# Row maxima taken one and a half groups ahead of the scores instead of two, in an attention and expert kernel

## The chip, the cores and the metric

The kernel runs on one core of a Trainium2 chip. The metric is device time in microseconds (us), from the start of the program to its end. Its engines work side by side and meet through semaphores: TensorE (PE, matmuls), VectorE (DVE), ScalarE (ACT), GpSimd (POOL), and SyncE (SP), which here only issues DMA transfers.

## The reference

Eight batches of 512 tokens with 256 features pass through a cross attention with 16 heads of 16, and then through a layer of eight experts of which each token takes two.

```python
q = _split_heads(_layernorm(x) @ wq.T + bq)
k = _split_heads(ctx @ wk.T + bk)
v = _split_heads(ctx @ wv.T + bv)
attn = softmax(einsum('bhqd,bhkd->bhqk', q, k) * 0.25)
x = x + einsum('bhqk,bhkd->bhqd', attn, v).reshape(B, S, 256) @ wo.T + bo
probs = softmax((_layernorm(x) @ Wg + bg) / 5.0)      # the two largest of 8, normalised: gates
h = gelu(_layernorm(x) @ W1[e] + b1[e])
x = x + sum_e gates[e] * (h @ W2[e] + b2[e])
```

## The kernel before

**Tiling.** The attention is cut into 32 groups, u = 0 to 31: eight batches i, and in each four groups g of four heads. A group is cut into eight slots, p = 0 to 7; a slot is two heads by one block of 128 keys (or queries) by 512. I write (g, p) for a slot of a batch, and batch and slot apart where both matter. The core's work for a group is done twice over:

- The **maxima pass**. `score` (L1448, the matmuls of L1457) puts the scores of 128 queries by 512 keys for two heads into one of three PSUM buffers (`ring`), and DVE's `reduce_max` (L1012) takes the negated row maxima into `negm`. When the group's eight slots are done, a unit called MT turns `negm` (PE, L1492), ACT copies it to `mT` (L903), and SP's `put_max` (L454, the DMA of L458) writes it into an extra row of the query stack `q_st`, 8 KB. The semaphore of that transfer is `m_in`.
- The **scores pass**. `score_t` (L1461, the matmuls of L1470) makes the transposed scores, and since the extra row is multiplied by a row of ones in `k_st`, they come out less the maximum. ACT takes the exponential into `probs` (L944), and `pv` (L1474, L1483) multiplies by the values. The first `score_t` of a group waits for `m_in`.

**What sets the order.** Each engine's program is written out by hand. In each slot PE does `score_t(u, p)`, then the maxima matmuls that `ahead(u, p)` names, then `pv` in slots 0, 2, 4 and 6, then the units that tables give for the slot. Before, `ahead` names slot p of group u + 2; in group 0 it names two in each of the first four slots, to catch up with the twelve made in the prologue (`EARLY`). The three PSUM buffers are handed round in the order of `ring_order`: a matmul pair may start only when the reader of the pair three places earlier is done, so in the steady order the scores of slot p wait for the DVE reduction of slot p - 2, and the maxima of slot p for the exponential of slot p - 1.

**Units.** The tables `PREP`, `NEXT`, `FIRST`, `POST` and `LAST_POST` put the other work into slots: XT and CT (transposes of the queries' and the context's input), K, Q, V (projections), OP (output projection of the batch before), XG and LG (transposes and logits of the routing), PX (ranks of the tokens among the experts' rows), CN (counts). Nearly all of them share one PSUM bank, `ps_x`, and each waits until the engine that empties it has taken the one before (`claim`). On DVE the tables `LN`, `LN2`, `ROUTE` and their LAST forms hold normalisation and routing. In the last batch DVE also makes tables for the expert stage (`first_tables`, L1228, in slots (2, 0), (2, 2) and (2, 4)), which end with `row_tab` (L1253). `row_tab` sets `tab_done`, and ACT waits for that before it copies XG0 to `xgT` (L910), because `xgT` lies in the same memory as the scratch of these tables. Two halves of a weight split (`low_w1`, L1195) stand between them on DVE, four more on POOL (L738).

**Queue of SP.** SP issues its transfers in program order and waits in that order: `put_max`, `load_stack` (k_st and q_st from HBM, L437), `store_parts` (K and Q to HBM, L451), `put_o` and `put_recip` (outputs and reciprocals), `fetch_o`, `load_kv`, `load_x`, weights.

**After the attention** 82 tiles of tokens run through the experts, bound to the order of `turn_x`, `hidden`, `turn_h` and `output` on PE (L1591 to L1627).

## Time and profile before

| | us |
|---|---|
| median of 3 runs | 833.87 |
| the three runs | 827.43, 833.87, 835.49 |
| the profiled execution | 829.04 |
| its span, first to last instruction | 827.3 |
| PE busy | 767.5 (93%) |
| DVE busy | 629.3 (76%) |
| ACT busy | 452.4 (55%) |
| POOL busy | 394.7 (48%) |
| attention: first score of group 0 to last `pv` | 40.2 to about 545 |

All times below count from the first instruction of the profiled execution; 1.7 us of its time lie outside the span. A row of the time line gives the start, the length from there to the end of the last instruction of the piece, the engine (SPq is SP's issuing queue), the line, the operation with what it writes and reads, the count, and in brackets how long the engine stood idle before it and what ended that. PE's matmuls are pipelined, so the next one starts some 0.1 us before the end shown.

### The profile page before, as it was taken

To read this page: it belongs to the slowest core of one execution; us is meant where nothing else is said; L and a number is where in the kernel's file an instruction comes from. 1 tells how busy PE (TensorE), PEld (TensorE's weight loads), DVE (VectorE), ACT (ScalarE), POOL (GpSimd) and SP (SyncE) were. 2 spreads that over 40 slices of the span, in tenths; PEclk is the share of its full clock that TensorE was granted. 3 is DMA by queue.
4 is the path that set the end of the run, shared out by engine and by line. 5 is a ranking of instruction groups with operands and counts; after the bars stand their busy time and mean duration, and the time that the engine had idled before them with its cause. 6 is when DMAs were issued, how large, how long until landed. Compare 5 with 4: busy or idle time off the path is not lost.

```text
span 827.3 us, 16330 instructions
## 1 busy us (share of the span) xinstructions
PE 767.5 (93%) x4698; PEld 459.5 (56%) x4698; DVE 629.3 (76%) x1131; ACT 452.4 (55%) x667; POOL 394.7 (48%) x358
## 2 busy tenths in 40 slices
PE   8599999999999999999999978678999989999995
PEld 4343434544434444444444423247989879998894
DVE  6786678798788798798778787866786887776674
ACT  2166676775775775776765655453345434444441
POOL 6506142446446456455425347654344455443444
PEclk9689999999999999999999979869999999999999
DMA  5766566567667667657467535263454456444441
GB/s 190 232 172 195 129 206 196 154 201 230 172 197 231 170 197 237 161 174 237 134 185 250 160 78 166 85 232 73 77 91 79 73 120 116 74 77 70 73 74 12
DMA packets 90285, 123.66 MB, mean 149 GB/s; under 512 B 15081, under 2 KB 52937, under 8 KB 89817
## 3 DMA queue, kind: packets, MB, share of 16 engines
q1 hardware_dynamic: 75832, 104.74, 43.2%
q0 software_dynamic: 13296, 17.09, 11.9%
q8 instruction: 43, 0.70, 0.4%
q10 hardware_dynamic: 1072, 0.79, 0.3%
q14 instruction: 42, 0.34, 0.2%
HBM read 64.96 MB, written 57.75 MB: 148 GB/s over the span
## 4 chain that ended last, share of the span: by engine, by line
PE 73%; DVE 10%; DMA 6%; issue 4%; ACT 2%; POOL 2%; SPq 0%; DVEq 0%; POOLq 0%; ACTq 0%
PE ps_pv L1483 14%; PE ring L1470 11%; PE ring L1625 9%; PE ring L1607 9%; PE ring L1457 7%; PE ps_x L1511 6%; DMA out<-y_sb,xs 5%; PE ps_x L1529 4%; DVE negm L1012 4%; PE ps_x L1501 3%; PE ps_x L1521 3%; PE ring L1616 3%; PE ps_x L1538 2%; PE ps_pv L1598 1%; ACT probs L944 1%
## 5 line engine op out<-in xcount | busy, mean ns | idle before, releaser
L1012 DVE TENSOR_REDUCE negm<-ring 128x2 f32<-128x1024 f32 x256 | 310.3, 1222 | 76.2 <-PE ring L1457 74.2
L944 ACT ACTIVATE probs<-ring 128x1024 f32<-128x1024 f32 x256 | 260.6, 1024 | 98.4 <-PE ring L1470 98.2
L845 POOL DMA_INDIRECT out<-y_sb,xs x71 | 110.3, 1554 | 138.3 <-DMA out<-y_sb,xs 82.6
L1483 PE MATMUL ps_pv<-probs,v_aug 128*32 128x512 f32 x1024 | 141.4, 625 | 5.3 <-ACT probs L944 5.2
L1470 PE MATMUL ring<-q_st,k_st 64*128 64x512 f32 x512 | 128.9, 503 | 6.5 <-DVE negm L1012 6.5
L1457 PE MATMUL ring<-k_st,q_st 64*128 64x512 f32 x512 | 110.7, 432 | 11.3 <-ACT probs L944 5.2
L1470 PEld LDWEIGHTS ring<-q_st,k_st 64*128 64x128 f32 x512 | 48.6, 188 | 107.7 <-issue 77.2
L973 ACT CAST xsT_hi<-ps_pv 128x256 fp32r<-128x256 f32 x71 | 26.4, 372 | 134.3 <-PE ps_pv L1598 134.3
L716 POOL DMA_INDIRECT xs_dram<-xg,rows x64 | 65.2, 1019 | 56.1 <-DVEq L1180 25.8
L1625 PE MATMUL ring<-w_hi,hT_hi 128*128 x284 | 85.7, 302 | 2.5 <-POOL w_lo L743 2.4
L1625 PE MATMUL ring<-w_lo,hT_hi 128*128 x284 | 80.3, 283 | 0.0
L1625 PE MATMUL ring<-w_hi,hT_lo 128*128 x284 | 79.8, 281 | 0.0
L785 POOL TENSOR_TENSOR v_aug<-v_flat,bv_sb 128x256 f32<-128x256 f32 x32 | 22.9, 733 | 99.5 <-PE ps_pv L1483 89.3
L1368 DVE TENSOR_TENSOR h_pre<-ring,b_sb 128x512 f32<-128x512 f32 x71 | 49.0, 690 | 25.6 <-PE ring L1607 24.2
L1607 PE MATMUL ring<-w_hi,xsT_hi 128*128 x142 | 59.6, 420 | 7.1 <-DVE xsT_lo L1356 6.9
L1457 PEld LDWEIGHTS ring<-k_st,q_st 64*128 64x128 f32 x512 | 50.9, 195 | 25.8 <-DVE negm L1012 8.9
L769 POOL CAST qk_hi<-qk 128x512 fp32r<-128x512 f32 x28 | 17.2, 613 | 89.2 <-ACT qk L897 58.5
L1607 PE MATMUL ring<-w_hi,xsT_lo 128*128 x142 | 57.1, 402 | 0.0
L1607 PE MATMUL ring<-w_lo,xsT_hi 128*128 x142 | 56.9, 401 | 0.0
L1625 PEld LDWEIGHTS ring<-w_hi,hT_hi 128*128 128x128 f32 x284 | 54.0, 190 | 2.9 <-issue 2.9
L1625 PEld LDWEIGHTS ring<-w_lo,hT_hi 128*128 128x128 f32 x284 | 54.0, 190 | 0.0
L1625 PEld LDWEIGHTS ring<-w_hi,hT_lo 128*128 128x128 f32 x284 | 53.8, 189 | 0.0
(194 smaller groups left out, 1236.6 us busy)
## 6 DMA issues: line engine op xcount, KB each, us to landing
k_st<-k_dram SPq DMA_DIRECT2D x64, 192.0 KB
q_st<-q_dram SPq DMA_DIRECT2D x64, 192.0 KB
xs<-xs_dram SPq DMA_DIRECT2D x71, 132.5 KB, 2.2
k_dram<-qk_hi SPq DMA_DIRECT2D x32, 256.0 KB, 2.4
q_dram<-qk_hi SPq DMA_DIRECT2D x32, 256.0 KB, 2.8
o_dram<-oT SPq DMA_DIRECT2D x32, 256.0 KB, 2.7
x_all<-in_x SPq DMA_DIRECT2D x8, 512.0 KB, 4.8
k_dram<-qk_lo SPq DMA_DIRECT2D x16, 256.0 KB, 2.3
```

Of the source, the lines that this page charges most:

```text
L716: pool.indirect_dma_start(out=xs_dram, out_offset=bass.IndirectOffsetOnAxis(ap=rows[:, k, t:t + 1], axis=0), in_=xg[:, t, :], in_offset=No ...
L845: pool.indirect_dma_start(out=out, out_offset=bass.IndirectOffsetOnAxis(ap=xs[j % AHEAD][:, TOKEN:TOKEN + 1].bitcast(I32), axis=0), in_=y_ ...
L944: nc.scalar.activation(probs[:, kt, 2 * jp:2 * jp + 2, :], ring[PLACE["ST", u, p] % RINGS][:], ACT.Exp).then_inc(exp_done, 1)
L1012: nc.vector.tensor_reduce(negm[:, v % 2, :, jp, kt], ring[PLACE["MX", v, p] % RINGS][:], AX.X, ALU.max, negate=True).then_inc(max_free, 1)
L1368: v.tensor_tensor(h_pre[:, j % 2, :], ps_h[j % 2], b1_sb[:, bass.ds(e, 1), :].rearrange("p o h -> p (o h)"), ALU.add).then_inc(f_h_out, 1)
L1457: mm = nc.tensor.matmul(ps[:, h, :], q_st[lo:lo + HALF, 2 * g + jp, kt * P:(kt + 1) * P], k_st[lo:lo + HALF, 2 * g + jp, :], start=True, s ...
L1470: mm = nc.tensor.matmul(ps[:, h, :], k_st[lo:lo + HALF, 2 * g + jp, kt * P:(kt + 1) * P], q_st[lo:lo + HALF, 2 * g + jp, :], start=True, s ...
L1483: mm = nc.tensor.matmul(ps_pv[2 * DH * j:2 * DH * (j + 1), :], v_aug[:, kt, HPG * g + j, :], probs[:, kt, j, :], start=(kt == 0), stop=(kt ...
L1511: mm = nc.tensor.matmul(ps[:, half], w[:, c, f * P:(f + 1) * P], act_t[:, c, half], start=(c == 0), stop=(c == DC - 1))
L1529: mm = nc.tensor.matmul(ps[:, (t % 2) * D:(t % 2 + 1) * D], numT[:, c, t * P:(t + 1) * P], wo_sb[:, c, :], start=(c == 0), stop=(c == DC - 1))
L1607: mm = nc.tensor.matmul(ps_h[j % 2], x[:, j % 2, c, :], w[:, bass.ds(e, 1), c, :].rearrange("p o h -> p (o h)"), start=(n == 0), stop=(n = ...
L1625: mm = nc.tensor.matmul(ps_y[j % 2][:, 0:D], h[:, j % 2, c, :], w[:, bass.ds(e, 1), c, :].rearrange("p o d -> p (o d)"), start=(n == 0), s ...
```

## The change

`ahead` now names slot p + 4 of group u + 1 in the first half of a group and slot p - 4 of group u + 2 in the second half, for every group, so that group 0 has eight maxima slots instead of twelve, and group 30 has four where it had none. MT of the next group stands in slot 4 instead of slot 0. The context's transposes CT0 and CT1 move from (3, 4) and (3, 6) to (3, 0) and (3, 2). In the first batch CT0, CT1 and XT0 move ahead, in the last batch OP2, OP3 and three normalisation steps move back by a slot or so. On SP `put_max` moves behind the transfers that stood after it.

```diff
-NEXT = {(2, 7): "XT0", (3, 1): "XT1", (3, 4): "CT0", (3, 6): "CT1"}
+NEXT = {(2, 7): "XT0", (3, 0): "CT0", (3, 1): "XT1", (3, 2): "CT1"}
-FIRST = {(0, 1): "CT0", (0, 2): "CT1", (0, 3): "K0a", (0, 4): "XT0", ...
+FIRST = {(0, 0): "CT0", (0, 1): "CT1", (0, 2): "XT0", (0, 3): "K0a", ...
-LAST_POST = {(1, 1): "OP0", (1, 3): "OP1", (1, 4): "OP2", (1, 5): "OP3",
+LAST_POST = {(1, 1): "OP0", (1, 3): "OP1", (1, 5): "OP2", (1, 6): "OP3",
-LAST_LN2 = {(1, 4): "stats0", (1, 6): "stats1", (1, 7): "sums"}
+LAST_LN2 = {(1, 5): "stats0", (1, 7): "stats1", (2, 0): "sums"}
...
-    if p == (2 if u == 0 else 0) and u + 1 < G:
+    if p == NP // 2 and u + 1 < G:
         out.append(("MT", u + 1))
...
 def ahead(u, p):
-    if u == 0:
-        rest = [(1, q) for q in range(NP // 2, NP)] + [(2, q) for q in range(NP)]
-        return rest[2 * p:2 * p + 2] if p < NP // 2 else rest[p + NP // 2:p + NP // 2 + 1]
-    return [(u + 2, p)] if u + 2 < G else []
+    v, q = (u + 1, p + NP // 2) if p < NP // 2 else (u + 2, p - NP // 2)
+    return [(v, q)] if v < G else []
...
-                put_max(i, 1)
...
                 if i > 0:
+                    put_max(i, 1)
                     fetch_o(i - 1, 1)
...
-                put_max(i, 2)
                 if more:
                     load_stack(i + 1, 0)
                 put_o(NG * i)
                 if more:
                     store_parts("Q", i + 1, 1)
+                if i > 0:
+                    put_max(i, 2)
+                if more:
                     store_parts("K", i + 1, 1)
...
-                put_max(i, 3)
...
                 put_recip(i, 0)
+                put_max(i, 3)
                 fetch_o(i, 0)
...
-                    put_max(i + 1, 0)
                     load_stack(i + 1, 2)
                 put_o(NG * i + 2)
+                if more:
+                    put_max(i + 1, 0)
```

Three places of the order follow. First PE in slots 0 to 3 of group 0, where ring<-k_st,q_st is a maxima matmul and ring<-q_st,k_st a scores matmul. Before:

```order
L1470 MATMUL ring<-q_st,k_st 128x512 x2
L1457 MATMUL ring<-k_st,q_st 128x512 x4
L1470 MATMUL ring<-q_st,k_st 128x512 x2
L1457 MATMUL ring<-k_st,q_st 128x512 x4
L1501 MATMUL ps_x<-ident,kv 128x128 x4
L1470 MATMUL ring<-q_st,k_st 128x512 x2
L1457 MATMUL ring<-k_st,q_st 128x512 x4
L1483 MATMUL ps_pv<-probs,v_aug 32x512 x4
L1492 MATMUL ps_x<-ident,negm 16x128
L1501 MATMUL ps_x<-ident,kv 128x128 x4
```

Of the change (its lines stand five lower in the file):

```order
L1475 MATMUL ring<-q_st,k_st 128x512 x2
L1462 MATMUL ring<-k_st,q_st 128x512 x2
L1506 MATMUL ps_x<-ident,kv 128x128 x4
L1475 MATMUL ring<-q_st,k_st 128x512 x2
L1462 MATMUL ring<-k_st,q_st 128x512 x2
L1506 MATMUL ps_x<-ident,kv 128x128 x4
L1475 MATMUL ring<-q_st,k_st 128x512 x2
L1462 MATMUL ring<-k_st,q_st 128x512 x2
L1488 MATMUL ps_pv<-probs,v_aug 32x512 x4
L1506 MATMUL ps_x<-ident,xn 128x128 x4
```

Each slot has lost one maxima pair, the transposes stand one or two slots earlier, and MT has left slot 2.

Second, SP from `put_recip` of the batch before (r_dram<-den) to the stacks of the next batch, in the first two groups of a batch. Before, the maxima's transfer (q_st<-mT) of group 1 has gone out ahead of these rows and that of group 2 is the seventh:

```order
L474 DMA r_dram<-den 128x32
L451 DMA k_dram<-qk_hi 128x512
L451 DMA k_dram<-qk_lo 128x512
L451 DMA k_dram<-qk_hi 128x512
L485 DMA numT<-o_dram 128x1x512
L490 DMA recT<-r_dram 128x1x512
L451 DMA q_dram<-qk_hi 128x512 x2
L451 DMA q_dram<-qk_lo 128x512
L458 DMA q_st<-mT 2x8x128
```

Of the change:

```order
L472 DMA r_dram<-den 128x32
L449 DMA k_dram<-qk_hi 128x512
L449 DMA k_dram<-qk_lo 128x512
L449 DMA k_dram<-qk_hi 128x512
L456 DMA q_st<-mT 2x8x128
L483 DMA numT<-o_dram 128x1x512
L488 DMA recT<-r_dram 128x1x512
L449 DMA q_dram<-qk_hi 128x512 x2
L449 DMA q_dram<-qk_lo 128x512
L435 DMA k_st<-k_dram 48x2x512 x2
```

The transfer of group 1 now stands right behind three stores of K, and that of group 2 has moved on behind stacks, output and the last stores of Q.

Third, DVE in the last batch, in slots (2, 0) to (2, 3), around the expert tables. Before:

```order
L1240 TENSOR_TENSOR done_n<-ends 128x7
L1195 TENSOR_TENSOR w_lo<-w_sb,w_hi 128x1024
L1242 TENSOR_TENSOR past<-tile_no,ends 128x328
L1243 TENSOR_TENSOR past_n<-past,done_n 128x328
L1244 TENSOR_REDUCE e_of<-past 128x41
L1245 TENSOR_REDUCE first_of<-past_n 128x41
L1195 TENSOR_TENSOR w_lo<-w_sb,w_hi 128x1024
L1044 RECIPROCAL den<-den 128x32
L1247 TENSOR_SCALAR e_tab<-e_of 128x41
```

Of the change:

```order
L1245 TENSOR_TENSOR done_n<-ends 128x7
L1017 TENSOR_REDUCE negm<-ring 128x2
L1200 TENSOR_TENSOR w_lo<-w_sb,w_hi 128x1024
L1017 TENSOR_REDUCE negm<-ring 128x2
L1247 TENSOR_TENSOR past<-tile_no,ends 128x328
L1248 TENSOR_TENSOR past_n<-past,done_n 128x328
L1249 TENSOR_REDUCE e_of<-past 128x41
L1250 TENSOR_REDUCE first_of<-past_n 128x41
L1017 TENSOR_REDUCE negm<-ring 128x2
L1200 TENSOR_TENSOR w_lo<-w_sb,w_hi 128x1024
L1049 RECIPROCAL den<-den 128x32
L1252 TENSOR_SCALAR e_tab<-e_of 128x41
```

Three maxima of group 31 stand between the table pieces, and a fourth ahead of them, in slot (2, 0).

## Rows read from the trace of the kernel before

**Rows 1.** Windows by stage: length, then PE, PEld, DVE, ACT, POOL busy, clock, DMA

```profile
180.00:240.00 60.00, 59.44 (x369) 27.05 (x367) 49.22 (x86) 40.91 (x56) 31.64 (x32) 1.00 0.66 197
473.00:511.00 38.00, 30.64 (x170) 11.66 (x169) 29.63 (x56) 18.64 (x23) 21.20 (x19) 0.82 0.42 121
511.00:546.00 35.00, 22.20 (x145) 7.85 (x142) 28.88 (x66) 19.27 (x24) 18.34 (x12) 0.86 0.40 137
```

**Rows 2.** PE's waits from 475 to 546 us: total us, times, longest

```profile
PE ps_x L1501 <- ACT xgT L910: 5.3, 1, 5.3
PE ring L1470 <- DVE negm L1012: 4.2, 3, 2.2
PE ps_x L1529 <- DVE numT L1048: 2.9, 1, 2.9
```

**Rows 3.** Time line of the first groups

```profile
37.73 9.14 DVE L1012 TENSOR_REDUCE negm<-ring 128x2 f32<-128x1024 f32 x8 [1.29 <-PE ring L1457]
40.23 0.79 PE L1470 MATMUL ring<-q_st,k_st 64*128 64x512 f32 x2 [0.43 <-DVE negm L1012]
45.39 1.12 PE L1501 MATMUL ps_x<-ident,kv 128*128 128x128 f32 x4
60.50 0.50 PE L1470 MATMUL ring<-q_st,k_st 64*128 64x512 f32 x2
```

**Rows 4.** Windows of PE alone: length, busy, granted clock, DMA share, GB/s

```profile
42.00:44.00 2.00, 1.66 (x8) 0.50 1.06 224
48.00:50.00 2.00, 1.65 (x13) 0.91 0.25 81
```

**Rows 5.** Time line of a middle batch, PE and SP

```profile
239.20 0.46 SPq L451 DMA_DIRECT2D k_dram<-qk_hi  x1
239.29 1.07 PE L1483 MATMUL ps_pv<-probs,v_aug 128*32 128x512 f32 x8
240.28 0.50 PE L1470 MATMUL ring<-q_st,k_st 64*128 64x512 f32 x2
240.62 0.40 PE L1457 MATMUL ring<-k_st,q_st 64*128 64x512 f32 x2
242.86 0.50 PE L1470 MATMUL ring<-q_st,k_st 64*128 64x512 f32 x2
252.58 0.46 SPq L451 DMA_DIRECT2D q_dram<-qk_lo  x1
258.72 0.49 PE L1470 MATMUL ring<-q_st,k_st 64*128 64x512 f32 x2
```

**Rows 6.** DMA issues, 236 to 245 us: KB each, us from issue to landing

```profile
k_dram<-qk_lo SPq DMA_DIRECT2D x1, 256.0 KB, 2.4
q_dram<-qk_lo SPq DMA_DIRECT2D x1, 256.0 KB, 6.6
r_dram<-den SPq DMA_DIRECT2D x1, 16.0 KB, 2.2
```

**Rows 7.** Time line of the last batch, group 30

```profile
510.61 0.74 DVE L1075 BATCH_NORM_STATS2 stats<-x_all 128x6 f32<-128x256 f32 x2
511.27 1.21 DVE L1012 TENSOR_REDUCE negm<-ring 128x2 f32<-128x1024 f32 x1
519.47 0.28 DVE L1247 TENSOR_SCALAR e_tab<-e_of 128x41 int32<-128x41 f32 x1
520.72 2.27 DVE L1250 TENSOR_TENSOR first_of<-tile_no,first_of 128x41 f32<-128x41 f32 x1
525.30 2.28 DVE L1253 SCALAR_TENSOR_TENSOR row_tab<-e_of,first_of 128x41 int32<-128x41 f32 x1
520.56 9.27 POOL L738 TENSOR_TENSOR w_lo<-w_sb,w_hi 128x1024 fp32r<-128x1024 f32 x4
527.68 0.58 ACT L910 COPY xgT<-ps_x 128x512 f32<-128x512 f32 x1 [7.76 <-DVE row_tab L1253]
528.33 1.12 PE L1501 MATMUL ps_x<-ident,xg 128*128 128x128 f32 x4 [5.30 <-ACT xgT L910]
```

## Prediction: what the change does to the time

> **What bounds the kernel now.** I read the windows by stage first. From batch 1 to batch 6 the reader sees PE busy for 59.4 of 60 us at the full clock (level 2.4 GHz), with DVE at 49, ACT at 41 and POOL at 32 [rows 1]. PE's work binds there, and a change that leaves that work alone and only shifts it can save at most the missing 0.6 us in 60. The last batch is different. From 473 to 511 us PE is busy for 31 of 38 us at a mean clock of 0.82, and from 511 to 546 for 22 of 35 at 0.86: here PE waits, and falls to the half level (1.2 GHz) between its waits. PE's waits of that part are, longest first, 5.3 us for ACT's copy to xgT, 4.2 us in three waits for a maximum on DVE, 2.9 us for the normalised outputs, again DVE [rows 2]. The 5.3 us are no matter of ACT: ACT had itself stood idle for 7.8 us until DVE ended row_tab [rows 7]. So in the last batch DVE's queue sets the pace, and in group 30 the path is DVE to row_tab, ACT's copy, PE's XG1. The beginning is a third case: eight reductions stand back to back from 37.7 us, 1.14 us each (9.14 by 8), the first scores wait for one of them, and group 0 takes from 40.23 to 60.50, 20.3 us [rows 3]. A middle group takes a quarter of the 60 us.
>
> **The change, part by part.** The sum of maxima slots stays at 256; four of them (4 x 2 matmuls, 4 reductions) leave slots 0 to 3 of group 0, and four come into slots 0 to 3 of group 30. All groups between have eight before and after. So there are two terms, of opposite sign, and one question about waits.
>
> *Start.* At the full clock a scores or a maxima pair costs PE 0.34 us (240.28 to 240.62), `pv` 1.0 (239.29 to 240.28), half a projection 0.95 (half of what lies between 240.96 and 242.86) [rows 5], and four transposes 0.56 (half of the 1.12 at the half level) [rows 3]. Group 0 after the change holds 16 pairs, three `pv`, four sets of transposes and three half projections: 5.4 + 3.0 + 2.2 + 2.9 = 13.5 us. Before it held four pairs more, 14.9 us, and took 20.3: 5.4 lost. Of these 4.1 are the half clock from 40.2 to about 48.4 (in 42 to 44 us the clock is 0.50, in 48 to 50 us it is 0.91 [rows 4]), and 1.3 are waits. The clock came back after PE had worked without a gap since the transposes at 45.39. Now CT0 stands in slot 0, where PE waited for DVE's second pair, and PE should be without gaps from about 42.4, which is 3 us earlier. If the clock comes back that much earlier, at 45, the half level costs 2.4 us, and with 1.0 of waits the group takes 16.9: 3.4 us saved. If it comes back at the same time as before, some 18.4: 1.9 saved. The lowest price is that of the four pairs alone, 1.4. I take 3.0, nearer to the upper end, since the clock follows the gaps in every row that I have.
>
> *Group 30.* Four reductions of 1.21 us [rows 7] come into DVE's queue between the end of group 29 and row_tab, which is 4.9 us. The move of OP3 by a slot brings one pair of layer norm statistics into it as well, 0.7 us [rows 7]. PE and ACT don't hide this, they are the ones who wait. Does DVE have a gap there that takes it up? No: from 511.27 to 527.58 its instructions stand without one. What can change the price is POOL. While POOL runs its four weight splits, from 520.56 to 529.83, DVE's small operations take as long as one of POOL's: first_of 2.27 us and row_tab 2.28, for 41 elements a partition [rows 7]. POOL starts about 2 us later now (its normalisation waits for DVE's sums, which come behind one reduction and the statistics), so it ends at about 531.8, and DVE, 5.6 us later, does its last eight table operations from 525.1 on: three of them under POOL at 2.27 each, to 531.9, then five in the open at the 0.28 of e_tab, to 533.3. So row_tab ends 5.6 us later; if the second split half and the reciprocal are slowed by POOL too, 6.9. I take 5.8 and keep 4.9 and 6.9. Everything behind the copy to xgT (XG1, logits, routing, the last scatter, the experts) keeps its order and moves with it.
>
> The Trainium skill, GPSIMD Engine Reference, section Key points, says that GpSimd shares its SBUF interfaces with VectorE and that the two get into each other's way when a DVE instruction has two SBUF inputs or is in a 2-port mode. The trace agrees, by the 2.27 us of first_of. By this rule the reductions, which read PSUM, would keep their 1.21 us under POOL, and the split half would not: that speaks for the upper end of this term.
>
> *Middle.* MT moves from slot 0 to slot 4, CT0 and CT1 take the two slots 4 and 6 places earlier, and every slot keeps about the sum it had. The order of the three buffers is the same. I put this at nothing; its cover is that PE has work in every slot, and at most 0.5 us a batch is there to be had. What is new is the time left to `put_max`. MT ended eight slots ahead of the first scores of its group, now four. In group 0 of a batch SP gets to it behind `put_recip` and three stores of K, the last issued from 239.20 to 239.66, and the scores that need it stand at 242.86 [rows 5]. It would be issued at 239.7, so it has 3.1 us to land. The rows nearest to it are 16 KB in 2.2 us and the store of K just ahead in 2.4 [rows 6], so 0.7 us remain. In group 1 it goes out behind the last store of Q (252.58 to 253.04) and is needed at 258.72: 5.7 us [rows 5], against 2.2 of the small transfer, or 6.6 of the slowest store of Q [rows 6]. In both I take the small transfer's 2.2 us, so no wait; the other end is in the rivals. Behind `put_max` on SP stand the fetches, each 0.6 us later, and DVE asks for those only many slots later. The earlier loads of the stacks get half a group more; no wait for them stands in the middle before, so that gives nothing.
>
> Sum: -3.0 + 5.8 + 0 = +2.8 us, from 829.04 to 831.8. The profiled execution stands 4.8 us below the median of the three runs, 833.87. The mean of all four is 831.5, and the same shift from there gives 834.3. I predict 834, about no change: work has gone from a place where it cost 3 to one where it costs nearly 6.
>
> **The rivals.**
>
> *Late maxima.* The 8 KB wait in the queue for the stores ahead of them. For it: 768 KB of K go out right ahead, and a store of Q landed only after 6.6 us [rows 6]. Against it: the store of K just ahead took 2.4. It decides from a landing of over 3.1 us in group 0. With 4.6 there, midway between 2.4 and 6.6, PE stands 1.5 us; with 6.6 in group 1 another 0.9 us; over six batches 14 us: 834.3 + 14 = 848, slower by 1.7%. The Trainium skill, DMA: Bandwidth & Descriptors, section Queues, rings and completion order, says that on each DMA engine the descriptors are consumed in the order of the ring. By this rule the 8 KB come behind all of the 768 KB, which is this rival; whether the wait gets long enough no row shows. Chance 0.16.
>
> *DVE's extra work is hidden.* The copy to xgT doesn't decide, or POOL's splits end before DVE's last operations and give back what the reductions cost (three operations at 2.3 us would fall to 0.28, -6 us). Against it: POOL starts later too. Then only the start counts: 831.5 - 3 = 828.5. Chance 0.12.
>
> *The change doesn't do at the start what it should.* The clock comes back no earlier and other waits take the place of the four pairs. Then + 5.8 alone: 837. Chance 0.10.
>
> *The last batch loses its half clock.* With the work standing otherwise, PE's gaps from 473 to 511 us fall elsewhere. At a mean of 0.82 these 38 us lose 6.8 us to the clock [rows 1]; with the 4.2 us of waits for maxima [rows 2] the most is 11 us, and with the start and the tables 834.3 - 11 = 823. Against it: groups 28 and 29 keep their count of reductions and all of their routing on DVE. Chance 0.08.
>
> **How the numbers follow.** The forecast, within some 3 us of 834, has 0.54. About 1% (8.3 us) is what a measurement of this kernel tells from no change, since its own runs lie 8 us apart. Within it of 833.87 are the forecast, the hidden case and the lost start: 0.76. Slower by over 1%: the late maxima, 0.16. Faster by over 1%: the last batch's clock, 0.08. The range for 8 in 10 takes in 828.5 and 837 with the bounds of the terms (start 1.4 to 3.4, tables 4.9 to 6.9) and the scatter of the runs: 826 to 843.
>
> **What would show it.** Right if group 0 runs in 17 to 18.5 us and the clock is full before 46 us; if the middle windows keep PE at over 59 of 60 us with no wait for DMA at L1475; and if, counted from the first scores of group 28, row_tab ends 5 to 7 us later than before. Wrong if PE waits at the first scores of a group (late maxima), if row_tab's delay is under 4 us (hidden), or if a middle batch changes its length by more than 0.5 us, which no term of mine explains.

## The result and the profile after

The changed kernel takes 837.38 us, the median of 9 runs (835.1 to 840.23), against 833.87 of before in 9 runs (827.43 to 835.9). The ratio, by which all differences here are told, is 1.0056 with a 95% interval of 1.0032 to 1.008 (the two medians alone give 1.0042, inside it): slower by 0.3 to 0.8%, which is within 1%, as forecast (834, range 826 to 843). Its profiled execution took 838.08 us with a span of 836.4. That of before, 829.04, was a quick one among its runs, so the two traces lie 9.1 us apart where the ratio gives 4.7. I come back to those 4 us.

Lines of the changed kernel stand five lower in the file than those of before (L1012 is L1017), those of SP's queue two higher (L458 is L456), and in the experiments they are a little further off. First the windows by stage, with the columns of [rows 1]; the last stage is 5 us longer than in [rows 1] and the clock in it 0.67 in place of 0.86. Part of that is no work of the change: in the start alone, an experiment below that keeps the last batch of before, the clock from 511 to 551 us is 0.69 as well. In the middle window PE is busy for 58.65 of 60 us, where the prediction wanted over 59.

```profile
120.00:180.00 60.00, 59.98 (x350) 26.87 (x352) 47.12 (x79) 40.70 (x55) 22.08 (x24) 0.97 0.57 172
180.00:240.00 60.00, 58.65 (x368) 27.08 (x361) 49.17 (x80) 41.30 (x55) 31.04 (x32) 1.00 0.65 198
473.00:511.00 38.00, 29.93 (x165) 11.62 (x164) 28.73 (x53) 18.76 (x23) 21.29 (x19) 0.78 0.27 87
511.00:551.00 40.00, 27.72 (x134) 9.94 (x135) 31.94 (x63) 18.09 (x22) 16.87 (x11) 0.67 0.36 119
```

**The start** is as forecast. Its time line answers to [rows 3], the two windows of PE alone to [rows 4]:

```profile
39.82 0.80 PE L1475 MATMUL ring<-q_st,k_st 64*128 64x512 f32 x2 [0.42 <-DVE negm L1017]
41.59 1.11 PE L1506 MATMUL ps_x<-ident,kv 128*128 128x128 f32 x4
57.29 0.50 PE L1475 MATMUL ring<-q_st,k_st 64*128 64x512 f32 x2
```

```profile
42.00:44.00 2.00, 2.00 (x9) 0.50 1.07 226
46.00:48.00 2.00, 2.00 (x16) 0.88 1.11 335
```

CT0 now stands at 41.59 in what was a gap, PE is busy for all of 42 to 44 us, the clock is back before 48, and group 0 takes 17.5 us instead of 20.3.

**The middle** is not. Here are PE's waits from 180 to 473 us, of the changed kernel (total us, times, longest):

```profile
PE ps_x L1497 <- DVE negm L1017: 4.8, 5, 1.2
PE ring L1462 <- ACT probs L949: 1.4, 2, 0.7
PE ps_x L1516 <- DVE row_of L1174: 0.3, 2, 0.2
```

and of the kernel before:

```profile
PE ring L1470 <- DVE negm L1012: 1.8, 4, 0.5
PE ring L1457 <- ACT probs L944: 1.4, 2, 0.7
```

MT (L1497) waits once in each batch, in slot (1, 4). The time line of one batch, DVE and PE, shows what it waits for:

```profile
248.39 1.11 DVE L1179 TENSOR_TENSOR row_k<-row_of,oh 128x32 f32<-128x32 f32 x1
250.32 3.57 DVE L1017 TENSOR_REDUCE negm<-ring 128x2 f32<-128x1024 f32 x3
249.41 1.06 PE L1488 MATMUL ps_pv<-probs,v_aug 128*32 128x512 f32 x8
251.69 0.27 PE L1497 MATMUL ps_x<-ident,negm 128*16 128x128 f32 x1 [1.22 <-DVE negm L1017]
```

DVE takes out the ranks of PX from slot (1, 2) on and then runs three reductions back to back. MT needs the first of the three, that of slot (1, 3). Before, the scores of the next slot had to wait for DVE at the same place, but only 0.5 us.

**Group 30** answers to [rows 7]:

```profile
524.52 9.81 DVE L1200 TENSOR_TENSOR w_lo<-w_sb,w_hi 128x1024 fp32r<-128x1024 f32 x1
535.45 0.20 DVE L1255 TENSOR_TENSOR first_of<-tile_no,first_of 128x41 f32<-128x41 f32 x1
535.91 0.20 DVE L1258 SCALAR_TENSOR_TENSOR row_tab<-e_of,first_of 128x41 int32<-128x41 f32 x1
523.97 9.27 POOL L743 TENSOR_TENSOR w_lo<-w_sb,w_hi 128x1024 fp32r<-128x1024 f32 x4
536.22 0.59 ACT L915 COPY xgT<-ps_x 128x512 f32<-128x512 f32 x1 [9.31 <-DVE row_tab L1258]
536.86 1.12 PE L1506 MATMUL ps_x<-ident,xg 128*128 128x128 f32 x4 [6.67 <-ACT xgT L915]
```

DVE's second split half takes 9.81 us, from just behind the start of POOL's four splits to just behind their end; elsewhere such a half takes 1.2 us. The table operations behind it are back at 0.2 us. Counted from the first scores of group 28, row_tab ends at 62.0 us (536.11 less 474.10), before at 53.95 (527.58 less 473.63): 8.1 us later. Only 6.8 of them lie behind the first scores of group 30.

| first scores of group, counted from those of group 0, after less before | us |
|---|---|
| 1 | -2.8 |
| 8 | -3.2 |
| 28 | +0.9 |
| 31 | +8.9 |
| last scores of group 31 | +11.1 |

So against this one execution of before the start gave 3 us, the middle took back 4, the tables 8, and group 31 another 2; behind the attention 2 of these came back, since the spans lie 9.1 us apart. The last of these steps is not the change's doing: group 31 of before was a quick one. From its first scores to its last it took 12.5 us there, 14.6 in the changed kernel, and 17.5 in the start alone, whose group 31 is the same work as before.

The other traces show how much such a reading is worth. From the first scores of group 8 to those of group 28, the stretch of the middle, the eight executions whose middle is that of before took 306.9 to 310.7 us (before itself 308.3), the four with the middle of the change 312.4 to 313.3. So the 4 us of the middle stand clear of the scatter; a difference of 2 us between two single traces would not.

### The profile page after: what moved, and what is told of

It is laid out like the page before. It is cut to its first block, busy times and chain, and to the rows that moved or that the text cites. A ratio compares the mean times of both kernels' runs of the same rounds, so it can differ in the third digit from the quotient of the medians.

```text
span 836.4 us, 16330 instructions
## 1 busy us (share of the span) xinstructions
PE 772.8 (92%) x4698; PEld 460.0 (55%) x4698; DVE 631.9 (76%) x1131; ACT 456.4 (55%) x667; POOL 393.1 (47%) x358
## 4 chain that ended last, share of the span: by engine, by line
PE 73%; DVE 10%; DMA 7%; issue 4%; ACT 2%; POOL 2%; SPq 1%; POOLq 1%; DVEq 0%; ACTq 0%
PE ps_pv L1488 14%; PE ring L1475 11%; PE ring L1612 9%; PE ring L1630 9%; PE ring L1462 7%; PE ps_x L1516 5%; DMA out<-y_sb,xs 5%; PE ps_x L1534 4%; DVE negm L1017 4%; PE ps_x L1506 3%; PE ps_x L1526 3%; PE ring L1621 3%; PE ps_x L1543 2%; PE ps_pv L1603 1%; DMA recT<-r_dram 1%
## 5 line engine op out<-in xcount | busy, mean ns | idle before, releaser
L1017 DVE TENSOR_REDUCE negm<-ring 128x2 f32<-128x1024 f32 x256 | 311.4, 1223 | 82.5 <-PE ring L1462 79.0
L1488 PE MATMUL ps_pv<-probs,v_aug 128*32 128x512 f32 x1024 | 146.1, 644 | 2.5 <-ACT probs L949 2.5
L1475 PE MATMUL ring<-q_st,k_st 64*128 64x512 f32 x512 | 132.3, 515 | 5.6 <-DVE negm L1017 5.6
L1475 PEld LDWEIGHTS ring<-q_st,k_st 64*128 64x128 f32 x512 | 49.7, 191 | 111.1 <-issue 82.7
```

The costliest lines, as they stand in the source:

```text
L1017: nc.vector.tensor_reduce(negm[:, v % 2, :, jp, kt], ring[PLACE["MX", v, p] % RINGS][:], AX.X, ALU.max, negate=True).then_inc(max_free, 1)
L1475: mm = nc.tensor.matmul(ps[:, h, :], k_st[lo:lo + HALF, 2 * g + jp, kt * P:(kt + 1) * P], q_st[lo:lo + HALF, 2 * g + jp, :], start=True, s ...
L1488: mm = nc.tensor.matmul(ps_pv[2 * DH * j:2 * DH * (j + 1), :], v_aug[:, kt, HPG * g + j, :], probs[:, kt, j, :], start=(kt == 0), stop=(kt ...
```

## The experiments

All comparisons are with the kernel before, run beside each experiment; a difference in us is one of ratios, with 0.001 for 0.83 us. Each ratio is uncertain by 0.002 to 0.0035, so a difference between two experiments by some 3 us. In the diffs, three dots stand for parts left out.

### The start alone

```diff
...
-    if u == 0:
-        rest = [(1, q) for q in range(NP // 2, NP)] + [(2, q) for q in range(NP)]
-        return rest[2 * p:2 * p + 2] if p < NP // 2 else rest[p + NP // 2:p + NP // 2 + 1]
-    return [(u + 2, p)] if u + 2 < G else []
+    return MAXIMA[u, p]
...
```

`MAXIMA` gives each slot one pair, and two in (1, 7), (2, 1), (3, 3) and (3, 5) of batch 0. The parts left out give batch 0 the unit tables, the place of MT and the order of `put_max` of the change.

> The kernel before with the first batch of the change alone: one maxima pair in a slot of group 0 in place of two, CT0, CT1 and XT0 ahead, MT of the next group in slot 4, and put_max in the order of the change. The four maxima pairs that group 0 no longer makes are made up in slots (1, 7), (2, 1), (3, 3) and (3, 5) of the first batch; from batch 1 on everything is the kernel before. My theory (the start saves 2.8 us of group 0, and the four pairs cost 4 x 0.34 = 1.4 us of PE where they now stand): faster than before by 1.4 to 2.8 us, and from the first scores of group 0 to those of group 4 1.4 to 2.8 us less. Rival (the gain of the start is only shifted into the rest of the first batch, where the DVE is as late as it was): no difference from before, under 0.5 us at the first scores of group 4.

830.99 us, ratio 0.9974 (0.9952 to 0.9997). In the trace group 0 is 2.2 us shorter, but at the first scores of group 4 only 0.2 us are left of it: the four pairs that were made up in batch 0 cost all of it there. Two later kernels with the same start agree: 0.1 and 0.2 us at group 4, 0.5 and 0.6 at group 8. The time says 2.2 us faster (0.3 to 4.0), the traces under 1, so what the start is worth by itself stays open between them. What is settled is that its gain in the changed kernel (2.8 us at group 1, 3.2 at group 8) exists because the four pairs are left out of batch 0, and that they have to be paid in some other place.

### The four reductions of group 30 alone

```diff
-    if p == (2 if u == 0 else 0) and u + 1 < G:
+    if p == (2 if u == 0 else NP // 2 if u == G - 2 else 0) and u + 1 < G:
...
+    if u == G - 3:
+        return [(u + 2, p)] if p < NP // 2 else []
+    if u == G - 2:
+        return [(u + 1, p + NP // 2)] if p < NP // 2 else []
     return [(u + 2, p)] if u + 2 < G else []
...
```

In the part left out `put_max` of group 31 moves behind `put_recip`.

> The kernel before with the end of the change alone: the last four maxima stand in the first half of group 30 instead of the second half of group 29, MT of group 31 in slot 4, its put_max behind put_recip; all else, LAST_POST and LAST_LN2 too, is the kernel before. My theory as the trace of the changed kernel has mended it: four reductions of 1.21 us come ahead of row_tab, the second split half on DVE falls into the four splits of POOL and is held until they end. Then row_tab ends 7 to 9 us later, counted from the first scores of group 28, that split half takes over 8 us instead of 1.2, and the time is 5 to 8 us above before. By the prediction's sum: row_tab 4.9 to 6.2 us later and no long split half. Rival (it was the shift of OP2, OP3 and the normalisation steps or the clock, not the reductions): under 3 us in both.

832.73 us, ratio 1.0001 (0.9976 to 1.0026): no change, and row_tab ends 3.1 us later (57.0 from the first scores of group 28). My theory and the prediction's sum both missed; the rival, that it was the shift and not the reductions, had said under 3 us in both, and came within 0.1 us. Time line of DVE, PE and POOL:

```profile
518.85 1.72 DVE L1249 TENSOR_TENSOR past<-tile_no,ends 128x328 f32<-128x328 f32 x1
520.60 2.53 DVE L1250 TENSOR_TENSOR past_n<-past,done_n 128x328 f32<-128x328 f32 x1
525.37 3.36 DVE L1202 TENSOR_TENSOR w_lo<-w_sb,w_hi 128x1024 fp32r<-128x1024 f32 x1
525.60 0.37 PE L1499 MATMUL ps_x<-ident,negm 128*16 128x128 f32 x1 [4.05 <-DVE negm L1019]
531.27 0.66 PE L1508 MATMUL ps_x<-ident,xg 128*128 128x128 f32 x4 [0.92 <-ACT xgT L917]
517.86 9.78 POOL L745 TENSOR_TENSOR w_lo<-w_sb,w_hi 128x1024 fp32r<-128x1024 f32 x4
```

Without the shift of the normalisation steps POOL starts its splits at 517.86, ahead of most of the table. They then hold three DVE operations for some 5 us in all, not one for 8.6, and end at 527.6; of the wait at XG1 0.9 us remain of 5.3. A new wait of 4.05 us at MT has come in its place.

### The whole end

The edit just shown and, with it, OP2, OP3 and the normalisation steps as in the change:

```diff
-LAST_POST = {(1, 1): "OP0", (1, 3): "OP1", (1, 4): "OP2", (1, 5): "OP3",
+LAST_POST = {(1, 1): "OP0", (1, 3): "OP1", (1, 5): "OP2", (1, 6): "OP3",
-LAST_LN2 = {(1, 4): "stats0", (1, 6): "stats1", (1, 7): "sums"}
+LAST_LN2 = {(1, 5): "stats0", (1, 7): "stats1", (2, 0): "sums"}
```

> The kernel before with the whole end of the change: the four reductions in group 30, as run alone, and with them OP2, OP3 and the three normalisation steps a slot or so later. The reductions alone left the time where it was (1.0001); the changed kernel stands 3.4 us above the same kernel with its end undone. Theory (the shifts bring DVE's split half to the point where POOL's four splits begin, so that it is held to their end): a split half of over 8 us, row_tab 7 to 9 us later than before, the time 2 to 5 us above before. Rival (it was the meeting with the middle, not the shifts): the split half stays under 4 us and the time within 1 us of before.

840.53 us, ratio 1.0066 (1.0033 to 1.01), 5.5 us slower; row_tab ends 5.6 us later (59.5). DVE, POOL and PE:

```profile
523.75 9.83 DVE L1202 TENSOR_TENSOR w_lo<-w_sb,w_hi 128x1024 fp32r<-128x1024 f32 x1
523.21 9.29 POOL L745 TENSOR_TENSOR w_lo<-w_sb,w_hi 128x1024 fp32r<-128x1024 f32 x4
536.12 1.11 PE L1508 MATMUL ps_x<-ident,xg 128*128 128x128 f32 x4 [6.69 <-ACT xgT L917]
```

So the four reductions alone don't bring the split half to the start of POOL's run, and with the shift they do. The shift reads like a detail of the diff, and adding it took the loss from nothing to 5.5 us. The shift without the reductions was not run. The twelve runs of this kernel lie further apart than those of the others (832.5 to 844.2 us), which nothing here explains.

### The change with its end undone

The start and middle of the change; the four pairs are caught up in batch 6, and batch 7 stands as before but for the order on SP.

```diff
...
-    if p == NP // 2 and u + 1 < G:
+    if p == (NP // 2 if u < G - NG else 0) and u + 1 < G:
...
```

> The changed kernel with its end undone: four maxima pairs are caught up in slots (1, 7), (2, 1), (3, 3) and (3, 5) of batch 6, and batch 7 has the maxima, MT, output projection and normalisation steps in the slots of the kernel before. Start and middle are those of the change. Each part alone, as run, gives -2.2 us for the start and 0 for the four reductions in group 30, while the whole change gives +4.7 against the 832.9 of before: some 7 us are in the middle or in how the parts meet. Theory (the middle costs 4 to 5 us by its waits at MT): 834.5 to 836, that is 1.5 to 3 us above before and 1.5 to 3 below the changed kernel. Rival (the middle costs nothing, as predicted, and the loss is the meeting of three late DVE pieces in the last batch): 830 to 831.5, as with the start alone.

834.02 us, ratio 1.0013 (0.9989 to 1.0037). That is 1.1 us above before and 3.3 above the start alone, and 3.6 below the changed kernel (1.0056 less 1.0013). The intervals are about 2 us wide to each side, so the point values decide only together with the traces. In that of this kernel MT waits 3.5 us in five batches, and from group 8 to group 28 it loses 4.9 us; the four traces with the middle of the change lose 4.1 to 4.9 there, the seven experiments without it -1.4 to +2.4. The middle costs 3 to 5 us.

```profile
PE ps_x L1511 <- DVE negm L1031: 3.5, 5, 1.2
```

### MT one slot later

MT of group 2 stands in (1, 5), in batches 2 to 7:

```diff
-    if p == NP // 2 and u + 1 < G:
+    if p == NP // 2 + (g == 1 and i > 1) and u + 1 < G:
```

> The changed kernel with MT of the next group in slot (1, 5) instead of (1, 4), for batches 2 to 7. In the changed kernel PE stands there for 0.6 to 1.2 us in each of these batches until DVE has made the maxima before it, 4.8 us in batches 2 to 6 together, right behind the ranks (PX) that DVE takes out in (1, 2). If it is MT that pays for this, the waits at MT are gone and the time falls by 3 to 5 us, as against the changed kernel. Rival (DVE is late there for everybody, and the scores of slots 5 and 6 wait instead, as they do in the kernel before): the waits move to the scores, at most 1 us in all is gained.

844.25 us, ratio 1.0127 (1.0097 to 1.0157): not faster but 5.9 us slower than the changed kernel. PE in the same batch:

```profile
254.00 0.51 PE L1475 MATMUL ring<-q_st,k_st 64*128 64x512 f32 x2 [1.06 <-DVE negm L1017]
255.75 1.13 PE L1534 MATMUL ps_x<-wo_sb,numT 128*128 128x256 f32 x4 [0.81 <-issue]
```

The wait has moved to the scores of the next slot, and MT now stands right in front of OP0, which needs the same bank ps_x and waits 0.8 us until ACT has emptied it. (The profile names ACT at one of these five waits and gives "issue", no releaser, at the other four.) The rival was right about the first, and nobody had the second. The waits of the five batches come to 2.3 us more than in the changed kernel, while this trace loses 5.6 us more from group 8 to group 28; the rest goes with a lower clock, 0.98 from 120 to 473 us against 0.99. So MT in (1, 4) is not itself the cause: DVE is late there, and whoever asks it next pays.

### DVE's split halves behind the tables

In the kernel before and in the changed kernel:

```diff
-LAST_LOW_W1 = {(2, 1): 6, (2, 3): 7}
+LAST_LOW_W1 = {(2, 5): 6, (2, 7): 7}
```

> The kernel before, with the two halves of the weight split on DVE (low_w1) moved from slots (2, 1) and (2, 3) to (2, 5) and (2, 7) of the last batch, that is behind the expert tables. If POOL's splits and the split halves are what the tables wait for, row_tab ends 6 to 8 us earlier than before (two halves of 1.2 us are gone from ahead of it, and it ends before or soon after POOL starts, so that the 2.3 us operations fall to 0.3), PE's wait of 5.3 us at XG1 is gone or under 1 us, and the time falls by 3 to 6 us; the split halves themselves may take up to 9 us behind the tables. Rival (the chain behind the tables, not the tables, is what the end waits for, or the held split half makes the later operations of DVE just as late): row_tab is earlier but the time changes by less than 1 us.

> The changed kernel with the same move: the two halves of the weight split on DVE in slots (2, 5) and (2, 7) of the last batch. If the 9.8 us split half is what made group 30 some 8 us later instead of 5.8, row_tab ends at least 8 us earlier than in the changed kernel and the time falls by 5 to 9 us, more than the same move brings in the kernel before. Rival (the four reductions alone set the delay): row_tab earlier by the 2.5 us of the two halves, and the time by about 2 us.

The kernel before with this edit: 831.35 us, ratio 0.9967 (0.9946 to 0.9988), row_tab 5.5 us earlier (48.5), a little under what was expected of both. The wait at XG1 is gone, and another has come: PE's longest wait for probs is 6.7 us, where it was 1.1. The changed kernel with this edit: 835.57, ratio 1.0028 (1.0005 to 1.005), 2.3 us below the changed kernel (within what two such ratios leave open), row_tab 3.5 us earlier. Here the rival came nearer, for a reason it did not name. DVE and POOL:

```profile
521.81 8.51 DVE L1252 TENSOR_SCALAR e_tab<-e_of 128x41 int32<-128x41 f32 x1
521.01 9.27 POOL L743 TENSOR_TENSOR w_lo<-w_sb,w_hi 128x1024 fp32r<-128x1024 f32 x4
```

With the split half gone, e_tab is held instead, 8.5 us for an operation of 0.28 us. So the size of the DVE operation is not what makes the hold long.

### POOL waits for row_tab

```diff
                 if i == B - 1:
+                    pool.wait_ge(tab_done, 1)
                     for e in range(2, E - 2):
                         low_w1(e)
```

In the changed kernel, in the kernel before, and in the kernel before with the start of the change:

> The changed kernel with one more wait: POOL begins its four weight splits of the last batch (L743) only when row_tab is made (tab_done). The tables are then made with POOL idle. If POOL's splits are what holds DVE's split half for 9.8 us, that half takes 1.2 us, row_tab ends 8 to 9 us earlier than in the changed kernel (at 53 to 54 us from the first scores of group 28), and PE's wait of 6.7 us at XG1 is under 1 us; the time falls by 3 to 7 us, less than row_tab gains, since POOL's splits now fall on the DVE's later steps and end some 4 us later. Rival (DVE itself is slow there, POOL only happens to run): the split half stays above 5 us and the time changes by under 1 us.

> The kernel before with POOL's four splits waiting for row_tab, and nothing of the change. With the start it gave 828.4, 4.8 us below before, of which 2.2 are the start's by its own run. If the two add, this one is 2 to 3.5 us below before, row_tab ends at 48 to 49 us from the first scores of group 28, and one routing operation of DVE (ld) is held for about 1.9 us later on. Rival (they help each other, since the half clock of group 31 hangs on both): under 1.5 us.

> A version meant to beat both: the kernel before with the start of the change alone (as run above, 2.2 us faster) and with POOL's four splits waiting for row_tab. In the kernel before three table operations take 2.3 us each under POOL's splits in place of 0.2, so row_tab should end 6 us earlier, at 48 to 49 us from the first scores of group 28. If the end waits for row_tab, the time is 824 to 828, 5 to 8 us below before. Rival (as with the weight split moved behind the tables, 5.5 us at row_tab give only 2 to 3 us of time, because POOL's splits then hold DVE's later steps): 827.5 to 830.

The changed kernel with the wait: 832.44 us, ratio 0.9992 (0.9969 to 1.0015), 5.3 us below the changed kernel. The split half takes 1.22 us, row_tab ends at 53.2, and the wait at XG1 is gone:

```profile
525.13 1.22 DVE L1201 TENSOR_TENSOR w_lo<-w_sb,w_hi 128x1024 fp32r<-128x1024 f32 x1
527.93 0.20 DVE L1259 SCALAR_TENSOR_TENSOR row_tab<-e_of,first_of 128x41 int32<-128x41 f32 x1
528.21 12.14 POOL L743 TENSOR_TENSOR w_lo<-w_sb,w_hi 128x1024 fp32r<-128x1024 f32 x4 [3.59 <-DVE row_tab L1259]
```

This shows the cause: DVE is held by POOL's run, not by its own work. The kernel before with the wait: 831.29, ratio 0.9979 (0.9959 to 1.0), 1.7 us faster and so between what the theory and the rival had said; its row_tab ends at 49.3, 4.7 us earlier, and ld is held for the 1.9 us that were expected. With the start as well: **828.36 us, ratio 0.994 (0.9909 to 0.997)**, 5 us below before and 9.7 below the changed kernel, and the lowest time of this study. The gains of the start (2.2) and of the wait (1.7) by themselves add up to 3.9, which is the same within the intervals. Its row_tab ends at 49.3. It is not the 8 us of the best case, and its trace shows the rival at work; DVE, POOL and PE:

```profile
521.83 0.20 DVE L1277 SCALAR_TENSOR_TENSOR row_tab<-e_of,first_of 128x41 int32<-128x41 f32 x1
532.39 1.89 DVE L1138 TENSOR_TENSOR ld<-lg,lmax 128x32 f32<-128x32 f32 x1
522.11 12.11 POOL L761 TENSOR_TENSOR w_lo<-w_sb,w_hi 128x1024 fp32r<-128x1024 f32 x4 [0.88 <-DVE row_tab L1277]
536.42 1.94 PE L1507 MATMUL ps_pv<-probs,v_aug 128*32 128x512 f32 x8 [4.75 <-ACT probs L968]
```

POOL's splits now take 12.1 us in place of 9.3, with DVE's later casts and splits running between them, and ld is held for 1.9.

### Two splits behind the scatter

```diff
-                    for e in range(2, E - 2):
+                    for e in range(2, 4):
                         low_w1(e)
...
                     scatter(i - 1)
+                    for e in range(4, E - 2):
+                        low_w1(e)
```

> The start of the change and POOL's wait for row_tab, as in the version that beat both, but two of POOL's four splits behind the scatter of batch 6. In that version PE waits 4.8 us for probs, ACT 5.4 us for the routing operation ld, and DVE for POOL's splits, two weight splits and ld together about 8 us. With only two splits there these waits shrink to under 2 us, and the time falls by another 2 to 4 us, to 825 to 826.5. Rival (the other two splits now fall into the end of the attention or the start of the experts, where PE needs all eight of them): no gain, or up to 4 us lost.

831.95 us, ratio 0.9974 (0.9953 to 0.9994): 2.8 us above the version it was made from, so the rival was right. The attention itself ends some 8 us earlier (last scores at 534.0, in the version it was made from at 542.5), and then PE stands before the first expert matmul:

```profile
547.10 4.64 POOL L761 TENSOR_TENSOR w_lo<-w_sb,w_hi 128x1024 fp32r<-128x1024 f32 x2
551.88 0.79 PE L1633 MATMUL ring<-w_hi,xsT_hi 128*128 x1 [13.96 <-POOL w_lo L761]
```

POOL stood idle for 11.6 us in front of that scatter. A version that used those for the two splits might keep part of the 8 us; it was not run.

### Maxima that are really late

The changed kernel, with put_max of group 1 behind the fetches and the stores of Q:

```diff
                 if i > 0:
-                    put_max(i, 1)
                     fetch_o(i - 1, 1)
                 if more:
                     store_parts("Q", i + 1, 0)
+                if i > 0:
+                    put_max(i, 1)
```

> The changed kernel with put_max of group 1 behind the fetches and the first stores of Q in batches 1 to 7: the rival of the late maxima, made to happen. In the changed kernel it is issued at 238.65 and the scores that need it stand at 241.31 without a wait; here it is issued at about 241.7. If a landing takes 2.2 us as the 16 KB beside it did, PE waits 2.5 to 3.5 us at the first scores of group 1 in each of batches 1 to 6, and the time is 15 to 22 us above the changed kernel, 852 to 860. If it queues behind the stores ahead of it, 6 to 7 us a batch and over 870. Rival (the scores have slack elsewhere and PE catches up): under 5 us.

867.6 us, ratio 1.0407 (1.0372 to 1.0441), 29 us above the changed kernel; more than the 15 to 22 of my own theory, less than the other end. SP and PE, and PE's waits from 180 to 490 us:

```profile
252.08 0.56 SPq L456 DMA_DIRECT2D q_st<-mT  x1
256.77 0.79 PE L1476 MATMUL ring<-q_st,k_st 64*128 64x512 f32 x2 [5.12 <-DMA q_st<-mT]
```

```profile
PE ring L1476 <- DMA q_st<-mT: 23.5, 5, 5.4
```

The 8 KB take 4.7 us from their issue (252.08 to 256.77), not 2.2: they have 512 KB of fetches and three stores of Q ahead of them. The row of the scores behind the wait is 0.79 us long, as at the half level, against 0.50 in a middle batch of before [rows 5]. The Trainium skill, DMA: Bandwidth & Descriptors, section Queues, rings and completion order, says that each DMA engine takes descriptors in ring order; the 4.7 us agree with that, but one later landing doesn't show it. In the changed kernel itself put_max goes out at 238.65 and the scores of group 1 start at 241.31 without a wait, so it landed within 2.7 us there, behind the 768 KB of K. No matmul of L1475 waits for a DMA in any batch, but this was near: the weight load (PEld) of these very scores names the transfer as what came last. Its 0.76 us of idle stand in another batch too, without a releaser, so no time was lost:

```profile
241.31 0.19 PEld L1475 LDWEIGHTS ring<-q_st,k_st 64*128 64x128 f32 x2 [0.76 <-DMA q_st<-mT]
```

## Why the prediction came out as it did

**The time.** Within 1% of before, inside the range, and the two terms have the signs that I gave them. The sum was +2.8 us; the ratio gives +4.7 (2.7 to 6.7). That it comes this near is in part luck: in group 30 a wrong working led to the right size, and the middle, where a step failed, is small.

**Start, -3.0.** Right: 2.8 us in group 0, with the full clock before 48 us as against about 48.4, and PE without gaps from 41.59 on. The test "full clock before 46" was missed by a little: 44 to 46 us is still at the half level, 46 to 48 at 0.88. A slip of the sum changes nothing: with the same 1.0 us of waits the second case gives 18.6 us for the group, not 18.4. What the start is worth by itself is less sure, since its four pairs have to be paid elsewhere; I had booked that payment under group 30.

**Group 30, +5.8.** The path (DVE, row_tab, ACT's copy, XG1) and the size of the loss were right for the end as a whole: 5.5 us in time and 5.6 at row_tab, run by itself. In the changed kernel row_tab was 8.1 us later, beyond my upper bound of 6.9 and the 5 to 7 of my test; 6.8 of these lie in group 30 and 1.2 in the two groups before it. The 1.2 may be scatter: in the six experiments whose work in these two groups is that of before, they took 0.1 to 2.6 us longer than in the execution that I compare with. The 6.8 are firm, since in all three traces with the tables of before row_tab ends 16.7 to 16.8 us behind the first scores of group 30, and they lie inside my bounds. But the working was wrong in its middle: "three of them under POOL at 2.27 each, to 531.9, then five in the open". No operation of the tables was slowed to 2.27 in the changed kernel. The split half, for which together with the reciprocal I had allowed at most another 1.1 us, was held for all of POOL's 9.3, and everything after it ran in the open. POOL itself began 2.9 us later, counted from group 28, where I had taken 2. I had carried over the pattern of [rows 7], one DVE operation let through after each of POOL's, as if it were a price by the operation. And the part of the diff that I costed at 0.7 us, the shift of OP3 and the statistics, was what, on top of the reductions, brought the half there; the four reductions by themselves made row_tab 3.1 us later and cost no time that could be measured (1.0001, 0.9976 to 1.0026).

**Middle, 0.** This step failed. "I put this at nothing; its cover is that PE has work in every slot": PE's work is no cover for a unit that stands in PE's own order and waits. MT needs the maxima of the slot just before it, in slot 4 as in slot 0; but slot (1, 4) lies behind the PX of (1, 2), for which DVE does seven small operations, and slot (1, 0) doesn't. The waits grew from 1.8 to 5.1 us in five batches, and by time the middle cost 3.3. The text named the test that shows it, a middle batch longer by over 0.5 us: that was so (0.8 a batch from group 8 to group 28, waits and half clock together, though unevenly: 2.2 in the first, next to nothing in the last two).

**The rivals.** Late maxima: not in this kernel, whose transfer landed within 2.7 us where I had counted 3.1 to spare; how near that was the last experiment shows, where an issue 3 us later, behind more transfers, cost 29 us. I had taken 4.6 us as its midway landing, and the one in that experiment took 4.7; that the two are so near is chance, for the queue ahead was another one. Hidden DVE work: refuted for the change, near the truth for the reductions alone. A start that does nothing: refuted for group 0; by itself its worth is open. A better half clock in the last batch: it didn't come. From 473 to 511 us the clock was 0.78 in place of 0.82, and the 0.67 behind it is near the 0.69 and 0.70 of the start alone and of the change with its end undone, both with the last batch's work as before.

**The 4 us between the traces.** The windows show where the quick execution of before differs, first before in its group 31, then the start alone, whose group 31 is the same work, to behind the end of the attention:

```profile
529.00:542.00 13.00, 11.22 (x81) 4.61 (x79) 8.91 (x28) 9.13 (x12) 0.83 (x1) 0.84 0.48 143
```

```profile
529.00:563.00 34.00, 27.72 (x110) 13.09 (x111) 19.99 (x46) 16.98 (x22) 12.25 (x10) 0.50 0.45 152
```

One had the clock at 0.84 through group 31, the other at 0.50 from 529 to 563 us (in 529 to 542 it was 0.51). Group 31 up to the last scores then took 12.5 us (529.37 to 541.87) and 17.5 (530.79 to 548.31). That these 5 us also make the spread of 8 us among the runs of one kernel is likely, and not shown.

## What to carry to other kernels

When a unit moves to another slot, ask who is late in that slot, not only whether the slot has room: the price was in DVE's queue behind the ranks, two slots earlier. Where two engines hold each other up, a shift of one slot can turn three short holds into one long one; so before costing such a stretch, take the other engine's run out of it with one wait, as here, where in the changed kernel that wait gave back 5.3 us, as much as the change had cost. Work that is merely moved from a cheap place must be priced where it lands.

## What the runs showed of the hardware

POOL's two-input operations, four in a row without a gap, can hold a single DVE operation to the end of all four: 9.81, 9.83 and 8.51 us, the last for 41 elements a partition with one input, and 9.82 us with MT one slot later. In the kernel before and in the start alone DVE got through after each one (2.27 us, three times in a row), and with the reductions alone it got through after each one again (1.72, 2.53, 3.36). DVE's reductions from PSUM kept their 1.2 us throughout. The Trainium skill, SBUF — State Buffer, section Who interferes with whom, says that whichever of the two issues first has the shared port pair for its whole instruction and the other blocks. The 2.27 us agree with that; the 9.8 us go beyond it, for there the hold was four instructions long. What decides between the two patterns is open. In both DVE arrives after POOL has begun, and how long after doesn't tell them apart: 0.54 to 0.80 us in the four long holds, but 0.16 us in the kernel before, 0.99 with the reductions alone and 1.75 with the late maxima, where DVE got through each time. Nor do the program's slots decide alone: the kernel with the late maxima has the last batch of the change but for the place of one transfer, and there the split half took 1.68 us and three small operations behind it were held for 2.1 to 2.4 each:

```profile
556.38 10.25 POOL L744 TENSOR_TENSOR w_lo<-w_sb,w_hi 128x1024 fp32r<-128x1024 f32 x4
558.13 1.68 DVE L1201 TENSOR_TENSOR w_lo<-w_sb,w_hi 128x1024 fp32r<-128x1024 f32 x1
560.00 2.08 DVE L1253 TENSOR_SCALAR e_tab<-e_of 128x41 int32<-128x41 f32 x1
562.11 4.58 DVE L1222 TENSOR_SCALAR need_up<-first_of 128x41 int32<-128x41 f32 x2
```

Counted from the first scores of group 30 row_tab ended at 22.1 us there, against 23.5 in the changed kernel and 16.7 before: one long hold and several short ones cost about as much.

A landing of 8 KB on SP's queue was within 2.7 us behind 768 KB of stores and took 4.7 us behind 512 KB of fetches and 768 KB of stores.
